# 32-head attention stage of a decoder kernel: first output product in two halves in two slots, keys of the next batch sorted two slots sooner

## The reference

```python
qkv = x @ Wqkv
q = qkv[..., :2 * Hx].reshape(Bx, 2 * NQ, Sx, HD)
k = qkv[..., 2 * Hx:2 * Hx + G].reshape(Bx, NKV, Sx, HD)
v = qkv[..., 2 * Hx + G:].reshape(Bx, NKV, Sx, HD)
k = jnp.repeat(k, 2 * NQ // NKV, axis=1)
v = jnp.repeat(v, NQ // NKV, axis=1)
scores = jnp.einsum('bhqd,bhkd->bhqk', q, k) / math.sqrt(HD)
scores = jnp.where(causal, scores, -jnp.inf)
aw = jax.nn.softmax(scores, axis=-1)
aw = aw.reshape(Bx, NQ, 2, Sx, Sx)
aw = aw[:, :, 0] - lam * aw[:, :, 1]
attn = jnp.einsum('bhqk,bhkd->bhqd', aw, v) * (1.0 - LAMBDA_INIT)
attn = jnp.transpose(attn, (0, 2, 1, 3)).reshape(Bx, Sx, Hx)
y = attn @ Wproj
y = jnp.transpose(y, (0, 2, 1)).reshape(Bx, Sx, Hx)
return y @ Wproj
```

## Time and profile before

| | |
|---|---|
| median of 3 runs | 2752.08 us (2749.12 to 2754.55) |
| the profiled execution | 2760.98 us, its span 2759.3 us |
| PE busy over the span | 2433.1 us (88%) |
| DVE, POOL, ACT busy | 1932.2 (70%), 1558.9 (56%), 1434.9 us (52%) |
| mean granted clock of PE | 0.945 |
| first attention stage | from the start to about 710 us |
| one step of it, from one y_hi to the next | 38.15 us where nothing disturbs it |

### The profile page before, as it was taken

How to read it: one execution, slowest core, us unless ns; L and a number is a source line. 1 busy time by engine, 2 the same in 40 slices (tenths; PEclk the granted TensorE clock), 3 DMA queues, 4 the chain that set the end, 5 groups by cost and what they waited for, 6 DMA issues and landing times. The chain is left out here.

```text
span 2759.3 us, 67851 instructions
## 1 busy us (share of the span) xinstructions
PE 2433.1 (88%) x25528; PEld 2026.7 (73%) x25528; DVE 1932.2 (70%) x3095; ACT 1434.9 (52%) x2255; POOL 1558.9 (56%) x1873
## 2 busy tenths in 40 slices
PE   5999999998699996998999994888896799997998
PEld 4677667766566764988999993677775577765998
DVE  2677667777377876344888885999985377775776
ACT  2566556655256664323665663656563355553333
POOL 3666566665344542055666665777755477763433
PEclk9899999999699998899999997999997899998999
DMA  8555556651677772024666663111001877851111
GB/s 201 129 148 151 131 145 152 146 131 37 180 185 195 198 202 72 16 96 149 220 229 221 216 217 118 37 41 47 22 13 31 238 192 210 214 140 35 58 57 50
DMA packets 228043, 363.58 MB, mean 132 GB/s; under 512 B 52720, under 2 KB 157168, under 8 KB 220272
## 3 DMA queue, kind: packets, MB, share of 16 engines
q1 hardware_dynamic: 207248, 281.31, 38.8%
q0 software_dynamic: 17376, 78.13, 8.1%
q10 hardware_dynamic: 3200, 1.05, 0.2%
HBM read 231.72 MB, written 133.69 MB: 132 GB/s over the span
## 5 line engine op out<-in xcount | busy, mean ns | idle before, releaser
L1285 ACT ACTIVATE self_probs<-self_score_ps 128x768 f32<-128x768 f32 x256 | 208.1, 813 | 201.2 <-PE self_score_ps L1187 199.2
L1501 POOL TENSOR_SCALAR_AFFINE_SELECT self_probs<-self_probs 128x512 f32<-128x512 f32 x256 | 167.3, 655 | 199.1 <-ACT self_probs L1285 198.7
L1422 DVE TENSOR_REDUCE self_neg_max<-self_max_ps 128x2 f32<-128x256 f32 x256 | 107.9, 422 | 204.0 <-PE self_max_ps L88 203.8
L730 DVE TENSOR_REDUCE cross_neg_max<-cross_max_ps 128x4 f32<-128x1024 f32 x128 | 156.0, 1222 | 77.6 <-PE cross_max_ps L509 76.6
L640 ACT ACTIVATE cross_probs<-cross_score_ps 128x1024 f32<-128x1024 f32 x128 | 131.1, 1024 | 96.7 <-PE cross_score_ps L530 96.5
L1423 DVE TENSOR_REDUCE self_neg_max<-self_max_ps 128x2 f32<-128x512 f32 x256 | 174.2, 681 | 0.0
L2213 POOL TENSOR_TENSOR moee_h_lo<-moee_h,moee_h_hi 128x512 fp32r<-128x512 f32 x78 | 112.0, 1437 | 92.9 <-ACT moee_h_hi L1950 92.1
L1950 ACT ACTIVATE moee_h_hi<-moee_h 128x512 fp32r<-128x512 f32 x110 | 69.5, 632 | 182.0 <-DVE moee_h L2116 152.4
L3508 POOL TENSOR_TENSOR ffn_g_lo<-ffn_g_full,ffn_g_hi 128x512 fp32r<-128x512 f32 x64 | 82.2, 1284 | 129.0 <-ACT ffn_g_hi L3394 116.7
L640 ACT ACTIVATE causal_probs<-causal_score_ps 128x768 f32<-128x768 f32 x128 | 103.8, 811 | 95.4 <-PE causal_score_ps L530 95.3
L1187 PE MATMUL self_score_ps<-self_q_stack,self_k_stack 49*128 49x128 f32 (+1 forms) x1024 | 131.3, 335 | 24.4 <-ACT self_probs L1285 10.7
(11 more groups left out here) (500 smaller groups left out, 9668.0 us busy)
## 6 DMA issues: line engine op xcount, KB each, us to landing
self_q<-self_q_split SPq DMA_DIRECT2D x48, 512.0 KB, 3.4
self_q_raw<-self_q SPq DMA_DIRECT2D x32, 768.0 KB, 8.0
cross_stacks<-cross_qk SPq DMA_DIRECT2D x64, 384.0 KB, 6.5
causal_stacks<-causal_qk SPq DMA_DIRECT2D x64, 384.0 KB, 6.6
moe_y_tiles<-lasting_y_out SPq DMA_DIRECT2D x55, 256.0 KB
mid<-lasting_y_out SPq DMA_DIRECT2D x48, 256.0 KB, 2.2
x_tiles<-zeros SPq DMA_DIRECT2D x16, 624.0 KB, 5.2
moee_xT<-x_tiles SPq DMA_DIRECT2D x39, 256.0 KB
```

Of the source, the lines that this page charges most:

```text
L730: last = dve.tensor_reduce(neg_max[p][:, tile, :, col % 4, :], bank[:].rearrange("p a (q k) -> p a q k", q=QT), AX.X, ALU.max, negate=True)
L1285: nc.scalar.activation(probs[g % 4][:, a, :, P:], score_ps[:, :, P:], ACT.Exp, scale=HD ** -0.5).then_inc(prob_ready, 1)
L1422: dve.tensor_reduce(neg_max[:, tile, :, c, 0:1], bank[:, :, 0:P], AX.X, ALU.max, negate=True)
L1501: pool.affine_select(diagonal, diagonal, [[0, 2], [0, 2], [1, P]], ALU.is_ge, zero, base=0, channel_multiplier=-1).then_inc(prob_masked, 1)
```

## The change

`output_1` gets a parameter `half`. In slot 12 PE does the products of tiles 0 and 1 (12 matmuls), in slot 14 those of tiles 2 and 3 (12 matmuls), all adding into the same bank, and only the second half signals `y1_done`. The waits for the bank (`v_kept`, `r_ready`) stand in the first half; each half waits for its own two tiles of `o_hi` and `o_lo`. `sort_k` moves from POOL's slot 15 to its slot 13.

```diff
-            def output_1(st):
+            def output_1(st, half):
                 if not st.has(-1):
                     pe.wait_ge(w_lo_ready, 2)
-                if st.has(3):
-                    pe.wait_ge(v_kept, st.done(3))
-                elif st.has(-1):
-                    pe.wait_ge(r_ready, st.done(-1))
-                pe.wait_ge(ohi_ready, TILES * st.done(0))
-                pe.wait_ge(olo_ready, TILES * st.done(0))
-                rows_product(D, o_hi, o_lo, TILES, lambda k: (wo_hi[:, k, :], wo_lo[:, k, :]), y1_done)
+                if half == 0:
+                    if st.has(3):
+                        pe.wait_ge(v_kept, st.done(3))
+                    elif st.has(-1):
+                        pe.wait_ge(r_ready, st.done(-1))
+                n = st.at(0) * TILES + 2 * half + 2
+                pe.wait_ge(ohi_ready, n)
+                pe.wait_ge(olo_ready, n)
+                for q in range(QT):
+                    for k in (2 * half, 2 * half + 1):
+                        cols = slice(q * P, (q + 1) * P)
+                        last = product3(pe, misc[:, q * D:(q + 1) * D], (o_hi[:, k, cols], o_lo[:, k, cols]),
+                                        (wo_hi[:, k, :], wo_lo[:, k, :]), k == 0 and q == 0, k == TILES - 1,
+                                        skip_group_check=True)
+                if half:
+                    last.then_inc(y1_done, 1)
...
-                    if i == 14 and st.has(0):
-                        output_1(st)
+                    if i in (12, 14) and st.has(0):
+                        output_1(st, i // 2 - 6)
...
-                    if i == 15 and st.has(2):
+                    if i == 13 and st.has(2):
                         sort_k(st)
```

## The result

The changed kernel takes 2719.93 us (median of 4 runs, 2715.89 to 2720.25), against 2750.60 for the kernel before beside it (4 runs). The ratio is 0.9897, 95% interval 0.9882 to 0.9912: 1.0% faster, some 31 us. The profiled span went from 2759.3 to 2718.3 us. The forecast was 2727, the range 2716 to 2742; in gain, 25 us forecast and 30.7 measured. Of the runs of all ten kernels one, of the kernel with the loop written out, was slow (3018.35 us at a granted clock of 0.73), and ratios and medians leave it out. Each kernel has one profile.

The account below looks back on a forecast made before the run. PE was taken to bound the steady step. Gains of 16.2 (key wait), -0.5 (jumps), 6.8 (clock) and 2.6 (tail) sum to 25.1 us, so 2752.1 - 25 = 2727 us, range 2716 to 2742.

Parts of the forecast that it names:

- The wait for keys goes, at no cost on POOL: PE's slot 0: the 1.63 us wait for POOL's sorted keys goes, the sort ending three and a half us ahead.
- The split brings a wait for ACT's copy of 0.65 us, and a step of 36.7: PE's slot 15 idles 0.65 us for ACT's copy; 11 steps gain 1.47 us each, 16.2 in total.
- The steps with a jump lose 0.5 us: Three steps ending in a jump back: no gain, each ends 0.16 us later, -0.5 us together.
- A third of the clock's price stays: Five stretches at 1.2 GHz behind key waits cost 10.2 us; 6.8 comes back, bounds 0 and 10.2.
- Rival A: Low-clock stretches only change place and their cost does not come back: 2734 us, chance 0.22.
- The tail gives 2.6 us: At t = 15, twelve products run within PE's wait for the last `o_lo`: 2.6 us gained, lower bound 1.5.
- rival C: All five low-clock stretches go and the double one behind t = 4 becomes single: 2722 us, chance 0.12.
- the likeliest case: The main forecast of 2727 us, chance 0.50, with its own range of 2722 to 2733.
- DVE as kept up by its idle time per step: Slots 0 to 2: PE won't wait for DVE's maxima or exponentials, as these engines idle 8 to 14 us per step.

## Why the prediction was right, and where a size was off

*The wait for keys goes, at no cost on POOL.* Right: it is gone in every kernel with the sort in slot 13, and the sort ends 3.9 us ahead of its use (3.5 forecast).

*The split brings a wait for ACT's copy of 0.65 us, and a step of 36.7.* Right: 0.55 us, 14 times; 36.76, and the 0.36 us waits of slot 13 are gone. The experiment with the query sort in slot 12 shows that ACT's order is its cause, as the prediction's working had it. The six of the nine steps that had no stretch at the lower clock gained 1.38 to 1.54 us each, against 1.47.

*The steps with a jump lose 0.5 us.* They gained 1.1 in the profiles, since the unexplained waits at the jumps (8.8 against 9.8 us in total) and the lengths of the stretches behind them changed by more. The stretch behind t = 4 was double and became single (2.12 us gained), the one behind t = 8 became double (0.88 lost). At t = 6, where both profiles have a single one, the step lost 0.14 us; 0.16 was the forecast.

*A third of the clock's price stays.* Mis-sized: 6.8 of 10.2 us were counted, and all five stretches in steps without a jump went, so that three of eight were left where about five were forecast. Steps behind t = 2, 7 and 10 gained 3.14, 3.12 and 2.96 us, the undisturbed ones 1.38 to 1.54, so 1.4 to 1.8 for each stretch; t = 12 and 13 gained 8.3 where 2 x 1.47 + 3.15 + 1.75 = 7.8 was the whole. The 0.65 us wait was placed between 0.36 (never) and 1.47 (five of 11); the runs put 0.55 with "never". Rival A, by which nothing comes back, falls: in the same nine steps gaps of 1.39 to 1.48 us lowered the clock three times, gaps of 1.8 to 1.9 us seven times, gaps of 2.0 to 2.3 us eight times, and the 0.55 us wait never. The Trainium skill, page "TensorE: Matmul & The Clock Gate", section "Why this matters for your kernels", warns of gaps above some 3 us. These traces differ from it: here gaps well below that do it.

*The tail gives 2.6 us.* It gave 3.6. The term took 12 products at the lower clock off the path and left the other 12 there. With half of them done ahead, PE idles 2.82 us and not 4.45, and the other 12 ran at the full clock in the profile. They don't always: in the eight kernels with the product in halves they follow one another in 0.12 us in three, the changed kernel among them, in 0.21 in two (one is the query sort in slot 12, whose last distance of 25.12 us gives 2.5, as forecast), and between in three. So part of the 1.0 us is chance. Over all kernels this last distance was 23.90 to 25.12 us with the product in halves (eight kernels) and 27.60 and 26.82 with the product whole (two).

With these two terms at their measured size the sum is 16.2 - 0.5 + 10.2 + 3.6 = 29.5, against the 31.0 of the two profiles and the 30.7 of the medians; the 1.5 that is missing is what the steps at the jumps did otherwise, 1.1 + 0.5. That is nearly rival C's case, forecast at 2722, which is also where the likeliest case's own range ended; the time came 2 us below it.

*What the prediction left out.* Had only the sort moved, I would have forecast 36.5 us a step. The trace of before has DVE's `x_lo` ending only 0.55 us ahead of the second product, and the step was 37.0. The product in slot 12 makes PE wait for ACT, but it keeps PE so far behind DVE in slot 2 that the wait for `x_lo` doesn't arise. The prediction named DVE as kept up by its idle time per step; that was right for this kernel by 0.28 us only (`x_lo` ends at 396.14, the product starts at 396.42).

## What to carry to other kernels

Where an engine waits each round for work that another does last in its list, look at when that work could have run, not at how long it takes: the sort had its data since long and stood behind a masking that waited for the bound engine itself. After such a wait is gone, walk along the lists of all engines for some slots on: in the kernel before ACT's copy ended 0.96 us ahead of its use (401.22 against 402.18) and DVE's `x_lo` 0.55 us, and each took part of the gain until its order was changed too. A gap in the matmul engine costs more than its length when it lets the clock fall, so the long ones are worth removing first: gaps of 1.4 to 2.3 us brought such stretches here, and the key sort alone, with gaps of 0.36 and 0.34 us in a step, had none in its nine steps.

## What the runs showed that I had not expected

The clock reacts to gaps of 1.4 to 2.3 us in a step of 37 to 39 in a graded way, in three steps of nine, then seven, then eight, and in both places that were tried, slot 0 and slot 11. Each low stretch behind such a gap costs 1.4 to 1.8 us, nearly as much as the gap. Each count is from one profile, so the order is better known than the numbers.

A jump back of PE costs 2.75 to 4.00 us here and a low-clock stretch behind it, 15 us in total for three in the changed kernel.

The rest of the program, which is the same in all ten kernels, is not of one length: from the last `y_hi` of this stage to the end of the span the profiles have 2057.8 us (before), 2048.2 (changed), and 2042.5 to 2065.5 for the others. The changed kernel's profile gained 10 us there, its medians did not show it. Low-clock stretches that fall otherwise don't account for it: summed over this part, the time times what the granted clock lacks of full speed is 123 us before and 129 us changed. The cause stays open.
